# Cross-attention row maxima taken over two PSUM banks at a time: four banks for these scores, two for the transposed ones

## The chip, the cores and the metric

The kernel runs on one core of a Trainium2 chip. The core has five engines that work side by side: TensorE (PE in the profile, its weight loads PEld), VectorE (DVE), ScalarE (ACT), GpSimd (POOL) and SyncE (SP), which here only issues transfers. Matmul results go to PSUM, which has eight banks of 512 fp32 columns on 128 partitions. The metric is the device time of one launch in microseconds (us); less is better.

## What is computed

One decoder layer in fp32 on 4 sequences of 512 tokens and 512 channels: causal self-attention, cross-attention on a context of 512 tokens and 128 channels, and a feed-forward part with eight experts and a shared one. Each is added to its input. The change touches only the cross-attention:

```
def _L0_xattn_ref(q, k, v):          # q: layernorm(x), k = v = ctx_512
    H, KV = (32, 8)                  # 32 query heads on 8 key/value heads
    D = E // H                       # 16 channels a head
    qh = q.reshape(B, S, KV, G, D).transpose(0, 2, 3, 1, 4)      # G = 4
    kh = k.reshape(B, S, KV, D).transpose(0, 2, 1, 3)
    vh = v.reshape(B, S, KV, D).transpose(0, 2, 1, 3)
    scores = jnp.einsum('bkgsd,bktd->bkgst', qh, kh) / scale
    weights = jax.nn.softmax(scores, axis=-1)
    out = jnp.einsum('bkgst,bktd->bkgsd', weights, vh)
    return out.transpose(0, 3, 1, 2, 4).reshape(B, S, E)
x = x + _L0_xattn_ref(_layernorm(x, axis=-1), ctx_512, ctx_512)
```

## The kernel before

The program has three stages that follow each other: self-attention (four groups of heads), cross-attention, feed-forward. Each engine has its own instruction list, written out in full; semaphores order them against each other.

Cross-attention is cut into 32 items (`ITEMS`), one for each of 4 sequences and 8 key/value heads. An item has four query heads and four tiles of 128 tokens. The softmax needs, for each query row, the maximum over 512 keys, and this maximum is found in a pass of its own. So an item has two kinds of score matmuls. Sixteen matmuls of the first kind, written `s` (`score`, line 1180, rows `ps<-k,q` of the profile), put queries on partitions, one 128x512 block in one PSUM bank each. VectorE takes the row maximum of a block (`maximum`, line 1750, a 128x512 reduce to 128x1, `xmax`). GpSimd splits the maxima of an item into a high and a low part (`xm`, lines 986 and 989), TensorE turns them (the "m" turn), ScalarE copies them, and two transfers put them as extra rows under the queries. Sixteen matmuls of the second kind, written `st` (line 1293, rows `ps<-q,k`), then compute the scores again with keys on partitions and the maximum already subtracted; ScalarE takes the exponential of each block (line 1545, `xp`), and these feed the products with the values (`pv`, line 1303, four heads side by side, eight hardware instructions for each of the four `pv` of an item).

The order of work around the change is that of `cross_steps(m)`. An item has eight steps k = 0..7. A step has on TensorE: one `s`, two `st`, one `s`; behind that in steps 2, 4 and 6 a turn (the maxima of item m+1; in step 4 of every second item the queries; in step 6 the output of item m-2); and in the odd steps one `pv` of item m-1. The `s` run 28 blocks (`S_FIRST`) ahead, so the `s` in item m belong to items m+1 and m+2, and the last 28 blocks have no `s` beside them. The two heads of a pair lie on partitions 0 and 64, so an `s` and the `st` next to it can use the two halves of the array at the same time.

PSUM banks in this stage: `XST` = 0..2 for `st` (block n in bank n % 3), `XS` = 3..5 for `s` (block u in bank 3 + u % 3), 6 for `pv`, 7 for turns. A bank comes free in this way: before `s` number u TensorE waits until u-2 maxima are done (`s_xmax`), and before `st` number n until n-2 exponentials are done (`s_xe`). VectorE waits for the `s` of each block (`s_xs`), ScalarE for each `st` (`s_st`). Beside the maxima VectorE divides the outputs (lines 1898 and 1880, in step 6) and, in some items, normalises rows for the next sequence or for the feed-forward part (`norm_piece`: lines 198, 207, 217 to 220, 1735), one piece behind the maxima of a step. The first 28 `s` run in the self-attention stage, in banks of that stage, with one maximum each.

Of the kernel before, what the change touches and what calls it, by code (L numbers as in the profile page):

```python
# [6 lines left out]
P = 128  # L7
ALU = mybir.AluOpType
ACT = mybir.ActivationFunctionType
AX_X = mybir.AxisListType.X  # L10
# [265 lines left out]
def score_of(u):  # L276

    return u // 8 * 2 + u % 2, u % 8 // 2
# [136 lines left out]
def build(nc, x, ctx_in, w_qkv_t, w_proj_t, gate_t, w1_t, w2_t, w3_t, kinds, out):  # L415
# [11 lines left out]
    with ExitStack() as whole:  # L427
# [110 lines left out]
        s_back = [sem(f"s_back{n}") for n in range(8)]  # L538
        s_mix = sem("s_mix")
        H1, H2, HT, HY, TURN, LOGIT, RANK = 0, 1, 2, 3, 5, 7, 7  # L540
        XST, XS, XO, XT = 0, 3, 6, 7

        pa = ExitStack()

# [541 lines left out]
        def _(pe):  # L1086
# [85 lines left out]
            def score(u, bank):  # L1172

                m = u // S_UNITS
                if u % S_UNITS == 0:
                    pe.wait_ge(s_xk3[m % KV // (KV // 2)], 32 * (m // KV + 1))
                    pe.wait_ge(s_xq3[m % 4], 32 * (m // 4 + 1))
                h, i = score_of(u % S_UNITS)
                rows = half_of(h, X_PART)
                pe.matmul(ps[:, bank, :], q3[rows, m % 4, h // 2, i * P:(i + 1) * P].bitcast(F32R),  # L1180
                          k3[rows, m % KV, :].bitcast(F32R), start=True, stop=True).then_inc(s_xs, 1)
# [81 lines left out]
            def cross(m):  # L1263
                for op in cross_steps(m):
                    if op[0] == "t":
                        kind, n = op[1:]

                        at = X_TURNS.index((kind, n))
                        if X_TURNS[at - 1][0] == "o":
                            pe.wait_ge(s_od, X_TURNS[at - 1][1] + 1)  # L1270
                        else:
                            pe.wait_ge(s_ta, taken(*X_TURNS[at - 1]))
                        if kind != "o":
                            turn_up(kind, n)
                        else:
                            pe.wait_ge(s_oe, n + 1)
                            for i in range(TOK_TILES):
                                ins = turned(pe, ps[:, XT, i * P:(i + 1) * P], o_t[:, n % 2, i * P:(i + 1) * P],
                                             ident[:, :])
                            ins.then_inc(s_ot, 1)  # L1280
                    elif op[0] == "s":
                        u = op[1]
                        pe.wait_ge(s_xmax, max(S_FIRST, u - 2))
                        score(u, XS + u % 3)
                    elif op[0] == "st":
                        h, t, n = block_of(op[1])
                        if n == 0:
                            pe.wait_ge(s_m3[m % 2], 32 * (m // 2 + 1))
                        n += S_UNITS * m
                        if n >= 3:  # L1290
                            pe.wait_ge(s_xe, n - 2)
                        rows = half_of(h, X_ROWS)
                        pe.matmul(ps[:, XST + n % 3, :], k3[rows, m % KV, t * P:(t + 1) * P].bitcast(F32R),  # L1293
                                  q3[rows, m % 4, h // 2, :].bitcast(F32R), start=True, stop=True).then_inc(s_st, 1)
                    elif op[0] == "pv":
                        j, n = op[1], m - 1
                        if j == 0:
                            pe.wait_ge(s_vx, n // KV + 1)
                            if n:
                                pe.wait_ge(s_oe, n)  # L1300
                        pe.wait_ge(s_xe, S_UNITS * m - 2 * (TOK_TILES - 1 - j))
                        for h in range(XG):
                            ins = pe.matmul(ps[VW * h:VW * (h + 1), XO, :], vx[:, n // KV % 2, n % KV, j, :],  # L1303
                                            xp[:, n % 2, h, j, :], start=(j == 0), stop=(j == TOK_TILES - 1),
                                            tile_position=(0, VW * h))
                        if j == TOK_TILES - 1:
                            ins.then_inc(s_xpv, 1)
# [140 lines left out]
        def _(act):  # L1448
# [90 lines left out]
            def cross(m):  # L1539
                for op in cross_steps(m):  # L1540
                    if op[0] == "st":
                        h, t, n = block_of(op[1])
                        n += S_UNITS * m
                        act.wait_ge(s_st, n + 1)
                        act.activation(xp[:, m % 2, h, t, :], ps[:, XST + n % 3, :], ACT.Exp,  # L1545
                                       scale=X_SCALE).then_inc(s_xe, 1)
                    elif op[0] == "t" and op[1] != "o":
                        take_turned(op[1], op[2])
                    elif op == ("pv", TOK_TILES - 1):
                        act.wait_ge(s_xpv, m)  # L1550
                        act.copy(o_t[:, (m - 1) % 2, :], ps[:, XO, :]).then_inc(s_oe, 1)
# [86 lines left out]
        def _(dve):  # L1638
# [105 lines left out]
            def maximum(u, bank):  # L1744
                m = u // S_UNITS
                h, i = score_of(u % S_UNITS)
                if u % S_UNITS == 0 and m >= 2:
                    dve.wait_ge(s_ml, m - 1)
                dve.wait_ge(s_xs, u + 1)
                dve.tensor_reduce(xmax[:, m % 2, h % 2, h // 2, i:i + 1], ps[:, bank, :], AX_X, ALU.max,  # L1750
                                  negate=True).then_inc(s_xmax, 1)

            def low_turned(g, op, t):

                i = op[1] % TOK_TILES
                dve.wait_ge(s_te, turns_done(g, t) + 1)
                dve.tensor_tensor(ptl[:, i:4 * i + 1:3, :],  # L1757
                                  ps[:, T_BANK + (1 + t) % 2, 0:(i + 1) * P].rearrange("p (j n) -> p j n", n=P),
                                  pth[:, i:4 * i + 1:3, :].bitcast(F32), ALU.subtract).then_inc(s_tl, 1)
# [124 lines left out]
            def cross(m):  # L1884
                pending = None
                for op in cross_steps(m):
                    if op[0] == "s":
                        maximum(op[1], XS + op[1] % 3)
                    if op[0] in ("s", "end") and pending is not None:
                        divide(*pending)  # L1890
                        pending = None
                    if op[0] == "end" and m < ITEMS:
                        norm_piece(m // KV, m % KV, op[1])
                    if op[:2] == ("t", "o"):
                        n = op[2]
                        dve.wait_ge(s_ot, n + 1)
                        o = ps[:, XT, :].rearrange("p (g d) -> p g d", d=VW)
                        pending = n, count.mark(dve.reciprocal(xrec[:, :], o[:, :, XD]))
# [222 lines left out]
```

## Time and profile before

| what | us |
|---|---|
| time, median of 3 runs (lowest, highest) | 1870.25 (1852.72, 1870.81) |
| profiled execution, its own time | 1844.48 |
| its span, from the first to the last instruction | 1842.6 |
| PE busy / DVE busy / ACT busy in the span | 1731.1 / 1210.5 / 918.4 |
| DVE in the maxima of cross-attention (line 1750, 512 instructions) | 320.8 |
| ACT in the exponentials of cross-attention (line 1545, 512 instructions) | 273.4 |

The profile shows the profiled execution, which is one run. Busy time is the sum of instruction durations of an engine; the durations of two neighbours overlap at their ends, so that back to back they start closer together than one of them lasts. Matmul ends are modelled, so a busy PE is not PE at its peak. Starts of instructions are the surer thing to read.

### The profile page before, as it was taken

What the parts mean: (1) busy time and instruction counts of PE and PEld (TensorE: products, weight loads), DVE (VectorE), ACT (ScalarE), POOL (GpSimd) and SP (SyncE); (2) the same over time, 40 slices, a digit from 0 to 9 for tenths busy, and PEclk for the clock granted to TensorE, in tenths of its full rate; (3) what the DMA queues carried; (4) which work ended last, traced back from release to release, by engine and by line L of the source; (5) the groups of instructions that cost most, each with busy time, mean ns of one, the idle gap of its engine ahead of it and who ended that gap; (6) DMA issues with size and microseconds to landing.
All of it is one profiled execution on the core that took longest, in us unless ns stands there. A gap on an engine that the chain in (4) does not pass through costs nothing.

```text
span 1842.6 us, 26550 instructions
## 1 busy us (share of the span) xinstructions
PE 1731.1 (94%) x9753; PEld 1327.8 (72%) x9753; DVE 1210.5 (66%) x2477; ACT 918.4 (50%) x1937; POOL 182.5 (10%) x299
## 2 busy tenths in 40 slices
PE   5799999999999999998799999998899999999998
PEld 4688888888888888886533333333399999999997
DVE  6656666556655656666488999999245246766766
ACT  2444444444434444433167777787432136666641
POOL 1000000000000000002032323121012400000024
PEclk9899999999999999998679999999679999999999
DMA  4000100010000100004023444442201357878746
GB/s 149 1 1 7 29 1 24 1 29 7 24 1 7 29 2 23 1 2 124 1 86 88 135 124 137 128 133 72 89 10 67 129 186 273 300 270 299 267 150 227
DMA packets 103203, 167.21 MB, mean 91 GB/s; under 512 B 8324, under 2 KB 52356, under 8 KB 102308
## 3 DMA queue, kind: packets, MB, share of 16 engines
q1 hardware_dynamic: 97956, 148.74, 24.9%
q0 software_dynamic: 5120, 16.78, 2.7%
q8 instruction: 79, 1.29, 0.3%
q14 instruction: 48, 0.39, 0.1%
HBM read 116.15 MB, written 49.28 MB: 90 GB/s over the span
## 4 chain that ended last, share of the span: by engine, by line
PE 77%; DVE 18%; ACT 3%; issue 2%; POOL 1%; DMA 0%; POOLq 0%; ACTq 0%
PE ps L181 37%; DVE xmax L1750 9%; PE ps L187 8%; PE ps L1418 8%; PE ps L1224 7%; PE ps L1119 5%; PE ps L1303 4%; PE ps L1180 3%; PE ps L1293 2%; DVE nmax L1718 1%; DVE stats L198 1%; DVE al L1765 1%; PE ps L1354 1%; DVE probs L1726 1%; ACT ah L1523 1%
## 5 line engine op out<-in xcount | busy, mean ns | idle before, releaser
L1750 DVE TENSOR_REDUCE xmax<-ps 128x1 f32<-128x512 f32 x512 | 320.8, 683 | 39.4 <-PE ps L1180 38.7
L1545 ACT ACTIVATE xp<-ps 128x512 f32<-128x512 f32 x512 | 273.4, 603 | 102.8 <-PE ps L1293 101.8
L1478 ACT ACTIVATE probs<-ps,nmax 128x128 f32<-128x128 f32 (+3 forms) x256 | 135.9, 531 | 169.2 <-DVE nmax L1718 169.2
L1180 PE MATMUL ps<-k,q 48*128 48x512 f32 x512 | 207.7, 484 | 7.5 <-DVE xmax L1750 4.2
L1293 PE MATMUL ps<-q,k 50*128 50x512 f32 x512 | 200.5, 480 | 4.9 <-ACT xp L1545 4.9
L1180 PEld LDWEIGHTS ps<-k,q 48*128 48x128 f32 x512 | 87.0, 194 | 145.2 <-DVE xmax L1750 113.6
L1518 ACT CAST pth<-ps 128x128 fp32r<-128x128 f32 (+3 forms) x256 | 108.5, 424 | 89.8 <-PE ps L187 89.8
L1303 PE MATMUL ps<-xp,vx 128*32 128x512 f32 x1024 | 147.4, 652 | 0.8 <-issue 0.8
L1718 DVE TENSOR_REDUCE nmax<-ps 128x1 f32<-128x128 f32 (+3 forms) x256 | 123.6, 483 | 12.4 <-PE ps L1119 11.0
L1757 DVE TENSOR_TENSOR ptl<-ps,pth 128x128 fp32r<-128x128 f32 (+3 forms) x256 | 123.9, 484 | 0.0
L181 PE MATMUL ps<-w12h,x_h 128*128 128x352 f32 x568 | 121.2, 335 | 0.0
L1765 DVE TENSOR_TENSOR al<-ps,ah 128x512 fp32r<-128x512 f32 x64 | 44.3, 691 | 116.8 <-ACT ah L1523 116.8
L187 PE MATMUL ps<-ident,probs 128*128 128x128 f32 x640 | 113.6, 276 | 7.3 <-DVE ptl L1757 4.7
L181 PE MATMUL ps<-w12h,x_l 128*128 128x352 f32 x568 | 116.1, 327 | 0.0
L181 PE MATMUL ps<-w12l,x_h 128*128 128x352 f32 x568 | 115.6, 326 | 0.0
L181 PE MATMUL ps<-xh,wh 128*128 128x512 f32 x384 | 110.6, 411 | 2.1 <-DVE wl L1696 2.1
L1923 DVE TENSOR_TENSOR w12l<-w_raw,w12h 128x1408 fp32r<-128x1408 f32 x56 | 90.7, 1620 | 27.9 <-ACT w12h L1576 27.9
L1726 DVE TENSOR_SCALAR probs<-probs,rinv 128x128 f32<-128x128 f32 (+3 forms) x256 | 100.8, 394 | 9.1
L1293 PEld LDWEIGHTS ps<-q,k 50*128 50x128 f32 x512 | 81.8, 196 | 34.1 <-ACT xp L1545 24.5
L181 PE MATMUL ps<-xh,wl 128*128 128x512 f32 x384 | 105.5, 397 | 0.0
L187 PEld LDWEIGHTS ps<-ident,probs 128*128 128x128 f32 x640 | 82.1, 142 | 32.0 <-DVE probs L1726 7.0
L181 PE MATMUL ps<-xl,wh 128*128 128x512 f32 x384 | 104.6, 395 | 0.0
(191 smaller groups left out, 3550.6 us busy)
## 6 DMA issues: line engine op xcount, KB each, us to landing
w_raw<-in_w_t SPq DMA_DIRECT2D x56, 704.0 KB, 6.0
w_raw<-in_w_t SPq DMA_DIRECT2D x28, 768.0 KB, 5.9
q<-q_way SPq DMA_DIRECT2D x64, 192.0 KB, 3.2
rows_x<-w_raw SPq DMA_DIRECT2D x39, 256.0 KB, 3.4
mixed<-rows_x SPq DMA_DIRECT2D x39, 256.0 KB, 4.4
rows_y<-y_s SPq DMA_DIRECT2D x39, 256.0 KB, 5.5
q_way<-q_hi SPq DMA_DIRECT2D x32, 256.0 KB, 4.5
w_raw<-in_w_qkv_t SPq DMA_DIRECT2D x24, 256.0 KB, 2.9
```

The source lines that it names most:

```text
L181: last = pe.matmul(dst, lhs, rhs, start=(n == 0), stop=(n == len(pairs) - 1))
L187: return pe.matmul(dst, src, ident, start=True, stop=True, is_transpose=True)
L1180: pe.matmul(ps[:, bank, :], q3[rows, m % 4, h // 2, i * P:(i + 1) * P].bitcast(F32R), k3[rows, m % KV, :].bitcast(F32R), start=True, stop= ...
L1224: ins = pe.matmul(ps[:, O_BANK + h % 2, j * P:], v[:, b % 2, j, :], p[:, 4 * j:3 * j + TOK_TILES, :].rearrange("p i n -> p (i n)"), start= ...
L1293: pe.matmul(ps[:, XST + n % 3, :], k3[rows, m % KV, t * P:(t + 1) * P].bitcast(F32R), q3[rows, m % 4, h // 2, :].bitcast(F32R), start=True ...
L1303: ins = pe.matmul(ps[VW * h:VW * (h + 1), XO, :], vx[:, n // KV % 2, n % KV, j, :], xp[:, n % 2, h, j, :], start=(j == 0), stop=(j == TOK_ ...
L1418: ins = pe.matmul(ps[:, HY + n % 2, :], lhs, rhs, start=(step.opens and m == 0), stop=(step.closes and m == len(pairs) - 1))
L1478: act.activation(probs[u % 4][:, 0:w], ps[:, S_BANK + u % 2, 0:w], ACT.Exp, bias=nmax[:, u % 4:u % 4 + 1], accum_out=rsum[:, u % 4:u % 4 + ...
L1545: act.activation(xp[:, m % 2, h, t, :], ps[:, XST + n % 3, :], ACT.Exp, scale=X_SCALE).then_inc(s_xe, 1)
L1718: dve.tensor_reduce(nmax[:, u % 4:u % 4 + 1], ps[:, S_BANK + u % 2, 0:w], AX_X, ALU.max, negate=True).then_inc(s_max, 1)
L1750: dve.tensor_reduce(xmax[:, m % 2, h % 2, h // 2, i:i + 1], ps[:, bank, :], AX_X, ALU.max, negate=True).then_inc(s_xmax, 1)
L1757: dve.tensor_tensor(ptl[:, i:4 * i + 1:3, :], ps[:, T_BANK + (1 + t) % 2, 0:(i + 1) * P].rearrange("p (j n) -> p j n", n=P), pth[:, i:4 * ...
```

## The change

The two `s` of a step now go to two neighbouring banks, and one VectorE instruction (`two_maxima`, new) reduces both: input 128x2x512, output 128x2, and it counts `s_xmax` up by two. For this the `s` get four banks (2..5, block u in bank 2 + u % 4) and the `st` two (0 and 1, block n in bank n % 2). TensorE waits for maxima only before the first `s` of a step, for the same count as before. Before `st` number n it now waits until n-1 exponentials are done, one more than before. The first 28 maxima are still taken one at a time.

```diff
-        XST, XS, XO, XT = 0, 3, 6, 7
+        XST, XS, XO, XT = 0, 2, 6, 7
...
                     elif op[0] == "s":
                         u = op[1]
-                        pe.wait_ge(s_xmax, max(S_FIRST, u - 2))
-                        score(u, XS + u % 3)
+                        if u % 2 == 0:
+
+                            pe.wait_ge(s_xmax, max(S_FIRST, u - 2))
+                        score(u, XS + u % 4)
                     elif op[0] == "st":
                         h, t, n = block_of(op[1])
                         if n == 0:
                             pe.wait_ge(s_m3[m % 2], 32 * (m // 2 + 1))
                         n += S_UNITS * m
-                        if n >= 3:
-                            pe.wait_ge(s_xe, n - 2)
+                        if n >= 2:
+                            pe.wait_ge(s_xe, n - 1)
                         rows = half_of(h, X_ROWS)
-                        pe.matmul(ps[:, XST + n % 3, :], k3[rows, m % KV, t * P:(t + 1) * P].bitcast(F32R),
+                        pe.matmul(ps[:, XST + n % 2, :], k3[rows, m % KV, t * P:(t + 1) * P].bitcast(F32R),
                                   q3[rows, m % 4, h // 2, :].bitcast(F32R), start=True, stop=True).then_inc(s_st, 1)
...
-                        act.activation(xp[:, m % 2, h, t, :], ps[:, XST + n % 3, :], ACT.Exp,
+                        act.activation(xp[:, m % 2, h, t, :], ps[:, XST + n % 2, :], ACT.Exp,
                                        scale=X_SCALE).then_inc(s_xe, 1)
...
+            def two_maxima(u):
+
+
+                m = u // S_UNITS
+                h, i = score_of(u % S_UNITS)
+                if u % S_UNITS == 0 and m >= 2:
+                    dve.wait_ge(s_ml, m - 1)
+                dve.wait_ge(s_xs, u + 2)
+                bank = XS + u % 4
+                dve.tensor_reduce(xmax[:, m % 2, :, h // 2, i], ps[:, bank:bank + 2, :], AX_X, ALU.max,
+                                  negate=True).then_inc(s_xmax, 2)
...
                 for op in cross_steps(m):
-                    if op[0] == "s":
-                        maximum(op[1], XS + op[1] % 3)
+                    if op[0] == "s" and op[1] % 2:
+                        two_maxima(op[1] - 1)
```

How TensorE's list stands in steps 4 and 5 of item 1, before (`s` is line 1180, `st` line 1293, the turn line 187, `pv` line 1303):

```order
L1180 MATMUL ps<-k,q 128x512 [waits s_xmax]
L1293 MATMUL ps<-q,k 128x512 [waits s_xe] x2
L1180 MATMUL ps<-k,q 128x512 [waits s_xmax]
L187 MATMUL ps<-ident,ctx_p 128x128 [waits s_cp,s_ta]
L187 MATMUL ps<-ident,ctx_p 128x128 x3
L1180 MATMUL ps<-k,q 128x512 [waits s_xmax]
L1293 MATMUL ps<-q,k 128x512 [waits s_xe] x2
L1180 MATMUL ps<-k,q 128x512 [waits s_xmax]
L1303 MATMUL ps<-xp,vx 32x512 [waits s_xe]
L1303 MATMUL ps<-xp,vx 32x512 x3
```

The same place now (`st` is line 1295, `pv` line 1305):

```order
L1180 MATMUL ps<-k,q 128x512 [waits s_xmax]
L1295 MATMUL ps<-q,k 128x512 [waits s_xe] x2
L1180 MATMUL ps<-k,q 128x512
L187 MATMUL ps<-ident,ctx_p 128x128 [waits s_cp,s_ta]
L187 MATMUL ps<-ident,ctx_p 128x128 x3
L1180 MATMUL ps<-k,q 128x512 [waits s_xmax]
L1295 MATMUL ps<-q,k 128x512 [waits s_xe] x2
L1180 MATMUL ps<-k,q 128x512
L1305 MATMUL ps<-xp,vx 32x512 [waits s_xe]
L1305 MATMUL ps<-xp,vx 32x512 x3
```

No matmul has moved. The second `s` of a step has lost its wait, and the two waits for exponentials before the `st` stand where they stood, each for one exponential more.

VectorE's list from step 5 to the end of an item that normalises query rows, before (maxima are line 1750):

```order
L1735 TENSOR_SCALAR xn<-res,mv,rstd 128x4x8x16 [waits s_qt]
L1750 TENSOR_REDUCE xmax<-ps 128x1 [waits s_xs] x2
L1898 RECIPROCAL xrec<-ps 128x16 [waits s_ot]
L1880 TENSOR_TENSOR xo<-ps,xrec 128x256 [waits s_dve]
L1750 TENSOR_REDUCE xmax<-ps 128x1 [waits s_xs] x2
L1735 TENSOR_SCALAR xn<-res,mv,rstd 128x4x8x16
```

The same place now (maxima are line 1764):

```order
L1737 TENSOR_SCALAR xn<-res,mv,rstd 128x4x8x16 [waits s_qt]
L1764 TENSOR_REDUCE xmax<-ps 128x2 [waits s_xs]
L1912 RECIPROCAL xrec<-ps 128x16 [waits s_ot]
L1894 TENSOR_TENSOR xo<-ps,xrec 128x256 [waits s_dve]
L1764 TENSOR_REDUCE xmax<-ps 128x2 [waits s_xs]
L1737 TENSOR_SCALAR xn<-res,mv,rstd 128x4x8x16
```

Two reduces have become one with two outputs; everything else stands between the same steps as before.

## Rows read from the trace of the kernel before

**Rows 1.** Page, part 2: TensorE's granted clock in 40 slices of 46 us.
```profile
PEclk9899999999999999998679999999679999999999
```

**Rows 2.** Page, part 4: the chain that ended last, by line.
```profile
PE ps L181 37%; DVE xmax L1750 9%; PE ps L187 8%; PE ps L1418 8%; PE ps L1224 7%; PE ps L1119 5%; PE ps L1303 4%; PE ps L1180 3%; PE ps L1293 2%; DVE nmax L1718 1%; DVE stats L198 1%; DVE al L1765 1%; PE ps L1354 1%; DVE probs L1726 1%; ACT ah L1523 1%
```

**Rows 3.** Waits, 920 to 1316 us: waiter, awaited, us in total, times, longest.
```profile
PEld ps L1180 <- DVE xmax L1750: 109.7, 174, 1.7
...
ACT xp L1545 <- PE ps L1293: 101.1, 139, 17.6
```

**Rows 4.** Timeline of POOL, line 986, once an item: start, us, instruction, idle before.
```profile
922.69 0.22 POOL L986 TENSOR_TENSOR xm<-xmax,ones 128x16 fp32r<-128x16 f32 x1 [42.88 <-DVE xmax L1750]
...
977.50 0.22 POOL L986 TENSOR_TENSOR xm<-xmax,ones 128x16 fp32r<-128x16 f32 x1 [3.14 <-DVE xmax L1750]
...
1023.29 0.22 POOL L986 TENSOR_TENSOR xm<-xmax,ones 128x16 fp32r<-128x16 f32 x1 [2.40 <-DVE xmax L1750]
...
1073.34 0.22 POOL L986 TENSOR_TENSOR xm<-xmax,ones 128x16 fp32r<-128x16 f32 x1 [2.86 <-DVE xmax L1750]
...
1119.12 0.21 POOL L986 TENSOR_TENSOR xm<-xmax,ones 128x16 fp32r<-128x16 f32 x1 [2.86 <-DVE xmax L1750]
...
1237.88 0.21 POOL L986 TENSOR_TENSOR xm<-xmax,ones 128x16 fp32r<-128x16 f32 x1 [2.86 <-DVE xmax L1750]
...
1277.84 0.22 POOL L986 TENSOR_TENSOR xm<-xmax,ones 128x16 fp32r<-128x16 f32 x1 [4.74 <-DVE xmax L1750]
1291.13 0.22 POOL L986 TENSOR_TENSOR xm<-xmax,ones 128x16 fp32r<-128x16 f32 x1 [3.66 <-DVE xmax L1750]
```

**Rows 5.** Timeline, steps 4 to 7 of one item, 1064.4 to 1070.3 us.
```profile
1064.52 0.50 PE L1180 MATMUL ps<-k,q 48*128 48x512 f32 x1
...
1065.09 2.07 ACT L1545 ACTIVATE xp<-ps 128x512 f32<-128x512 f32 x4 [0.58 <-PE ps L1293]
...
1065.74 0.49 PE L1293 MATMUL ps<-q,k 50*128 50x512 f32 x1 [0.24 <-ACT xp L1545]
...
1066.23 1.07 PE L1303 MATMUL ps<-xp,vx 128*32 128x512 f32 x8
1067.22 0.50 PE L1180 MATMUL ps<-k,q 48*128 48x512 f32 x1
...
1068.48 0.50 PE L1180 MATMUL ps<-k,q 48*128 48x512 f32 x1
...
1070.15 0.50 PE L1180 MATMUL ps<-k,q 48*128 48x512 f32 x1
```

**Rows 6.** DVE: groups by form (busy us, mean ns), then two rows of its timeline.
```profile
L1750 DVE TENSOR_REDUCE xmax<-ps 128x1 f32<-128x512 f32 x512 | 320.8, 683 | 39.4 <-PE ps L1180 38.7
...
L1718 DVE TENSOR_REDUCE nmax<-ps 128x1 f32<-128x128 f32 x64 | 18.0, 282 | 0.0
...
1059.66 0.74 DVE L1735 TENSOR_SCALAR xn<-res,mv,rstd 128x512 f32<-128x512 f32 x1
...
1069.59 3.67 DVE L1750 TENSOR_REDUCE xmax<-ps 128x1 f32<-128x512 f32 x6
```

**Rows 7.** Timelines of PE and ACT in the last items, where no `s` is left.
```profile
1306.01 1.22 PE L1293 MATMUL ps<-q,k 50*128 50x512 f32 x3
...
1306.84 2.08 ACT L1545 ACTIVATE xp<-ps 128x512 f32<-128x512 f32 x4 [1.99 <-PE ps L1293]
...
1307.48 0.79 PE L1293 MATMUL ps<-q,k 50*128 50x512 f32 x1 [0.26 <-ACT xp L1545]
...
1308.21 1.94 PE L1303 MATMUL ps<-xp,vx 128*32 128x512 f32 x8
1310.07 1.22 PE L1293 MATMUL ps<-q,k 50*128 50x512 f32 x3
```

**Rows 8.** Windows: stretch, its us, busy PE, PEld, DVE, ACT, POOL, PEclk, DMA.
```profile
1264.00:1277.84 13.84, 11.96 (x69) 4.76 (x69) 13.63 (x33) 9.98 (x20) 2.13 (x4) 1.00 0.17 50
...
1292.00:1318.00 26.00, 24.97 (x91) 7.25 (x90) 2.49 (x8) 14.56 (x28) 2.08 (x3) 0.52 0.28 88
```

## The prediction, made before the changed kernel had run

> **What bounds the kernel now.** The chain that ended last comes first: 9% of the span is VectorE's maxima, and TensorE's cross-attention matmuls (lines 1180, 1293, 1303) stand beside them with 9% [rows 2]. So the stage is shared between VectorE and TensorE. The waits inside it agree: TensorE's weight loads stand 109.7 us behind maxima, in 174 places, while the exponentials have spare time, since ScalarE waits 101.1 us for the `st` [rows 3]. Taken alone this speaks for the change: it makes VectorE's work cheaper and gives up a bank where ScalarE seems to have time.
>
> The wait table overstates it, since a weight load also "waits" while the array is still busy with `pv`. The timeline of starts shows the truth. Two steps, from the `s` that opens an even step to the next such `s`, take 1067.22 - 1064.52 = 2.70 us where no turn is in them, and 1070.15 - 1067.22 = 2.93 us with a turn [rows 5]. In the first case one `st` was late because of an exponential, although it had three banks: the exponentials start 0.57 us behind the opening `s`, the first lasts some 0.60, and the fourth `st` starts at 1065.74, which is 0.57 + 0.60 + 0.05 = 1.22 behind 1064.52 [rows 5]. So the `st` ring already touches the path with three banks.
>
> How long items take is read from GpSimd's instruction that comes once an item [rows 4]. Four kinds: (a) quiet items, without normalising: 977.50 to 1023.29 and 1073.34 to 1119.12, four each, 11.45 us an item; 1119.12 to 1237.88 is one busy group and six more quiet ones at the same pace; 14 in all, at about two alternating lengths of which 11.45 is the mean. (b) Two busy groups of four, 50.05 us each (1023.29 to 1073.34). (c) The three before 1277.84, 39.96 us, with VectorE busy 13.63 of 13.84 us in the last of them [rows 8]. (d) The first four, 54.81 us, partly at half clock, one at the end (13.29), and behind it the tail without `s`.
>
> **The change part by part.**
>
> *The maxima.* A reduce of 128 columns takes 282 ns, one of 512 takes 683: 1.044 ns a column. A pair of 1024 columns would take 683 + 512 x 1.044 = 1.22 us. Six in a row of 512 span 3.67 us, so they start (3.67 - 0.68)/5 = 0.60 apart, and a pair should follow the next one after 0.60 + 0.53 = 1.13 us instead of 1.20 [rows 6]. The gain is 0.07 us a pair, 0.53 us of VectorE's time an item; for the 242 pairs 16 us if every bit were on the path. The Trainium skill, page "VectorE: DVE Perf Modes", section on the trn2 errata, has the same shape, a fixed cost and one cycle a column at 0.96 GHz; by it the pair saves only the fixed cost of one instruction, and the trace's slope agrees.
>
> *The waits of `s`.* A pair may only start when both `s` are there, some 0.34 us later than the first maximum did, and it frees two banks at once. With two pairs of banks this costs nothing in quiet items: pair p must end before the opening `s` of step p+2, which is a whole two-step (2.7 us or more) behind its own, and it ends 0.79 + 1.22 = 2.0 us behind that. I take zero.
>
> *The `st` ring, two banks for three.* This is the term that decides. Call T the opening `s` of an even step. The exponentials of its two `st` start at T + 0.57 and T + 1.06 (four of them span 2.07, so they start 0.49 apart) and end at T + 1.17 and T + 1.66 [rows 5]. With two banks the third `st` waits for the first exponential, T + 1.22, and the fourth for the second, T + 1.66 + 0.05 = T + 1.71. In the row of now `pv` starts 0.49 behind such a late `st` (1065.74 to 1066.23), since the late `st` and the last `s` no longer overlap their start-up with the step before, and the next opening `s` comes 0.99 behind `pv` (1066.23 to 1067.22). So a two-step takes 1.71 + 0.50 + 0.99 = 3.20 us, turn or no turn: a turn now ends at T + 1.26 [rows 5], within the time that the step waits anyway. Without a turn that is +0.50 against 2.70, with one +0.27 against 2.93. The `pv` in the odd step gives ScalarE 1 us to catch up, so the next even step starts without a debt. An item is 4 x 3.20 = 12.80 us, and 0.05 more for the copy of the output that delays the exponentials of step 0: 12.85, to be compared with 11.45. Behind the waiting `st` stand the last `s`, the pair maximum, the turn of the maxima and `pv`: all of TensorE's list shifts with it.
>
> *Quiet items:* 14 x (12.85 - 11.45) = **+19.6 us**.
>
> *Busy groups.* Without normalising they could not take less than 4 x 12.85 = 51.4; the normalising pieces of step 0 (three of four items have one) delay the pair of step 1 and with it the turn of the maxima, each by at most its own length, 0.74 for a query tile [rows 6]: 51.4 + 2.2 = 53.6. Now 50.05. VectorE has more room than before, so I take the middle, 52.5: 2 x 2.45 = **+4.9**.
>
> *The three items of (c):* bounds are 39.96 less 3 x 0.53 (VectorE sets the pace) and 3 x (12.85 + 0.74) = 40.8. Nearest to the upper end, since all three carry the same waits: **+0.6**. *First four and the one at half clock:* at half clock TensorE itself takes longer than the ring, and the first item has no `pv`; bounds 0 and 5 x 1.4; I take **+1.9**.
>
> *The tail.* At half clock four `st` start a two-step; the exponentials start 0.83 behind, the fourth `st` comes at 1.47, `pv` at 2.20, the next one at 4.06 [rows 7]. With two banks the third `st` moves to 1.47 and the fourth one exponential further, 1.96: +0.49 in each of four two-steps without a turn and about +0.2 in two with one: **+2.4**.
>
> Sum: 19.6 + 4.9 + 0.6 + 1.9 + 2.4 = **+29.4 us**. The profiled execution took 1844.48 us and would take about 1874. It lies 25.8 us below the median of the runs, 1870.25, and nothing in the trace says where that comes from; the same sum on the median gives **1900 us**.
>
> **The rivals.**
>
> *R1, faster: VectorE is the bound.* If the ring did not bind (if `st` found free banks because `pv` lies between), only the saved 0.07 us a pair would be left, 16 us, and up to 0.3 us an item of TensorE's waits for the second maximum of a step, 8 us: 1870 - 16 to -24, say 1850. For it: the 109.7 us of waits on maxima [rows 3] and stretches like 1264 to 1277.84 where VectorE is never idle [rows 8]. Against it: the four `st` of a two-step stand in front of its `pv`, not around it. It decides if the fourth `st` starts before T + 1.6.
>
> *R2, within 1%: the ring costs half.* If the late `st` keeps its overlap, `pv` follows 0.34 behind it (the distance of two pairs of matmuls), and busy stretches gain on VectorE what they lose on the ring: two-steps of 3.04, quiet items of 12.2, 14 x 0.75 = 10.5, the rest about 3: 1884.
>
> *R3, much slower: the clock falls.* The granted clock is at or near full speed in cross-attention except at its two ends [rows 1]; it is 0.52 in the tail [rows 8]. Now TensorE will pause in each two-step. At half clock a two-step takes 4.06 and more [rows 7]; if a third of 30 items ran so, 10 x 4 x 0.9 = 36 us come on top: 1936. Against it: items of 13.84 us, with longer pauses than the 12.85 forecast, ran at clock 1.00 [rows 8]. The Trainium skill, page "TensorE: Matmul & The Clock Gate", section on psum-queue depth-cycling, speaks against this change: a kernel whose TensorE idles briefly as it cycles through PSUM banks saw its clock swing between half and full. By that rule the time would be R3's; no run here shows it for pauses this short.
>
> **How the numbers follow.** The ring as worked out 0.75, R2 0.12, R1 0.06, R3 0.07. About 1% is what a measurement of this kernel can tell from no change, so slower means above 1889. Of the first case, whose own range is 1886 to 1915, a small part falls within 1%: slower 0.78, within 1% 0.17, faster 0.05. The range reaches down to R2, whose runs may also lie as low as the lowest one before, and up past the upper bounds of the open terms (busy groups +2.2, first items +5, a few items at half clock): 1872 to 1920.
>
> **What would show each step.** The pair maximum lasts 1.2 us, and VectorE's busy time in maxima falls by some 30 us. GpSimd's item mark comes every 12.8 to 12.9 us in quiet items. Waits of `st` (line 1295) for exponentials grow by some 30 to 40 us in total; waits of `s` for maxima shrink. All items alternate no longer, since a turn costs nothing. The clock stays 1.0 in quiet items. The prediction is wrong if quiet items stay below 12.2, if `pv` starts less than 2.1 us behind the opening `s`, if pairs take far over 1.3 us, or if the clock falls between 980 and 1240 us.

## The result

| | median us (lowest to highest) | runs |
|---|---|---|
| before | 1870.25 (1852.72 to 1870.81) | 3 |
| changed | 1896.45 (1892.38 to 1906.51) | 3 |
| ratio | 1.0192, 95% interval 1.015 to 1.0234 | |

The change makes the kernel slower, by 26 us between the medians. A second comparison on another occasion (e0 below) gave 1.0231 (1.0179 to 1.0283). The profiled execution of the changed kernel took 1892.38 us, with a span of 1890.5; that of before had 1842.6. The page of the changed kernel:

```profile
span 1890.5 us, 26515 instructions
...
PEclk9999999999999999996789999899898899999999
...
PE ps L181 35%; PE ps L187 9%; PE ps L1420 7%; PE ps L1224 7%; PE ps L1119 5%; PE ps L1305 5%; PE ps L1180 4%; PE ps L1295 4%; DVE xmax L1764 4%; DVE nmax L1720 1%; DVE al L1779 1%; PE ps L1356 1%; DVE probs L1728 1%; DVE stats L198 1%; DVE ptl L1771 1%
...
L1764 DVE TENSOR_REDUCE xmax<-ps 128x2 f32<-128x1024 f32 x242 | 295.4, 1221 | 67.5 <-PE ps L1180 66.0
```

The 242 pairs last 1221 ns each, as the slope of [rows 6] said, and the maxima's share of the chain fell from 9% [rows 2] to 4%. TensorE's cross-attention lines took over the share: 9% became 13%. VectorE's relief is small, though: its busy time in the maxima went from 320.8 us to 313.3 (295.4 in the pairs, 17.9 in the 28 single ones at the start), not down by some 30 us as forecast.

The item marks of GpSimd, to be held against [rows 4]:

```profile
918.45 0.22 POOL L986 TENSOR_TENSOR xm<-xmax,ones 128x16 fp32r<-128x16 f32 x1 [41.89 <-DVE xmax L1764]
...
978.31 0.22 POOL L986 TENSOR_TENSOR xm<-xmax,ones 128x16 fp32r<-128x16 f32 x1 [3.46 <-DVE xmax L1764]
...
1028.64 0.21 POOL L986 TENSOR_TENSOR xm<-xmax,ones 128x16 fp32r<-128x16 f32 x1 [2.85 <-DVE xmax L1764]
...
1081.58 0.21 POOL L986 TENSOR_TENSOR xm<-xmax,ones 128x16 fp32r<-128x16 f32 x1 [3.31 <-DVE xmax L1764]
...
1132.21 0.22 POOL L986 TENSOR_TENSOR xm<-xmax,ones 128x16 fp32r<-128x16 f32 x1 [3.32 <-DVE xmax L1764]
...
1190.08 0.21 POOL L986 TENSOR_TENSOR xm<-xmax,ones 128x16 fp32r<-128x16 f32 x1 [5.43 <-DVE xmax L1764]
...
1266.79 0.21 POOL L986 TENSOR_TENSOR xm<-xmax,ones 128x16 fp32r<-128x16 f32 x1 [3.31 <-DVE xmax L1764]
...
1320.05 0.21 POOL L986 TENSOR_TENSOR xm<-xmax,ones 128x16 fp32r<-128x16 f32 x1 [3.77 <-DVE xmax L1764]
```

| stretch between marks | before | changed | difference | forecast |
|---|---|---|---|---|
| first four items | 54.81 | 59.86 | +5.1 | +1.9 with the last item |
| quiet items, 14 | 160.3 | 177.7 | +17.4 | +19.6 |
| two busy groups of four | 100.1 | 110.8 | +10.7 | +4.9 |
| three items of (c) and the last one | 53.25 | 53.26 | 0.0 | +0.6 |
| all 30 intervals | 368.4 | 401.6 | +33.2 | |

The first mark comes 4.2 us earlier, and from the last mark to the end it is 570.5 us against 551.5, 19 us more. That last figure is not the change's, as e0 will show. In the quiet items one of 13.75 us is counted whose first part ran at half clock; without it the mean is 12.6 us.

How a two-step looks now, TensorE from 1093.7 to 1106.3 us:

```profile
1096.80 0.49 PE L1180 MATMUL ps<-k,q 48*128 48x512 f32 x1
1096.80 0.73 PE L1295 MATMUL ps<-q,k 50*128 50x512 f32 x2
...
1098.01 0.98 PE L1295 MATMUL ps<-q,k 50*128 50x512 f32 x2 [0.23 <-ACT xp L1547]
1098.50 0.50 PE L1180 MATMUL ps<-k,q 48*128 48x512 f32 x1
1098.93 1.07 PE L1305 MATMUL ps<-xp,vx 128*32 128x512 f32 x8
1099.92 0.50 PE L1180 MATMUL ps<-k,q 48*128 48x512 f32 x1
...
1103.06 0.50 PE L1180 MATMUL ps<-k,q 48*128 48x512 f32 x1
...
1106.25 0.49 PE L1180 MATMUL ps<-k,q 48*128 48x512 f32 x1
```

With T = 1096.80 the third `st` starts at T + 1.21, the fourth with the last `s` at T + 1.70, `pv` at T + 2.13, the next two-step at T + 3.12. The two that follow take 3.14 (a turn is in it) and 3.19 (none is, but the copy of the output). So a turn costs nothing any more, and an item is 12.58 us. `pv` stands 0.43 us behind the last score matmul (1098.50 to 1098.93).

### The profile page after: what moved, and what is told of

Its sections match the earlier page's. It is cut to its first block, busy times and chain, and to the rows that moved or that the text cites. A ratio compares the mean times of both kernels' runs of the same rounds, so it can differ in the third digit from the quotient of the medians.

```text
span 1890.5 us, 26515 instructions
## 1 busy us (share of the span) xinstructions
PE 1747.6 (92%) x9753; PEld 1323.9 (70%) x9753; DVE 1204.7 (64%) x2235; ACT 923.8 (49%) x1937; POOL 182.1 (10%) x299
## 4 chain that ended last, share of the span: by engine, by line
PE 78%; DVE 13%; issue 4%; ACT 3%; POOL 1%; another core or an unknown queue 1%; DMA 0%; DVEq 0%; POOLq 0%; ACTq 0%
PE ps L181 35%; PE ps L187 9%; PE ps L1420 7%; PE ps L1224 7%; PE ps L1119 5%; PE ps L1305 5%; PE ps L1180 4%; PE ps L1295 4%; DVE xmax L1764 4%; DVE nmax L1720 1%; DVE al L1779 1%; PE ps L1356 1%; DVE probs L1728 1%; DVE stats L198 1%; DVE ptl L1771 1%
## 5 line engine op out<-in xcount | busy, mean ns | idle before, releaser
L1764 DVE TENSOR_REDUCE xmax<-ps 128x2 f32<-128x1024 f32 x242 | 295.4, 1221 | 67.5 <-PE ps L1180 66.0
L1547 ACT ACTIVATE xp<-ps 128x512 f32<-128x512 f32 x512 | 278.8, 598 | 114.4 <-PE ps L1295 109.9
L1180 PE MATMUL ps<-k,q 48*128 48x512 f32 x512 | 217.6, 495 | 6.7 <-DVE xmax L1764 3.3
L1295 PE MATMUL ps<-q,k 50*128 50x512 f32 x512 | 217.9, 491 | 6.0 <-ACT xp L1547 5.8
L1305 PE MATMUL ps<-xp,vx 128*32 128x512 f32 x1024 | 142.9, 633 | 0.8 <-issue 0.8
L1720 DVE TENSOR_REDUCE nmax<-ps 128x1 f32<-128x128 f32 (+3 forms) x256 | 123.3, 482 | 12.1 <-PE ps L1119 10.7
L1295 PEld LDWEIGHTS ps<-q,k 50*128 50x128 f32 x512 | 86.5, 193 | 57.4 <-ACT xp L1547 54.2
L181 PEld LDWEIGHTS ps<-w12h,x_h 128*128 128x128 f32 x568 | 96.1, 192 | 16.2 <-issue 9.5
```

The lines of the kernel that those rows point to most:

```text
L181: last = pe.matmul(dst, lhs, rhs, start=(n == 0), stop=(n == len(pairs) - 1))
L1295: pe.matmul(ps[:, XST + n % 2, :], k3[rows, m % KV, t * P:(t + 1) * P].bitcast(F32R), q3[rows, m % 4, h // 2, :].bitcast(F32R), start=True ...
L1547: act.activation(xp[:, m % 2, h, t, :], ps[:, XST + n % 2, :], ACT.Exp, scale=X_SCALE).then_inc(s_xe, 1)
L1720: dve.tensor_reduce(nmax[:, u % 4:u % 4 + 1], ps[:, S_BANK + u % 2, 0:w], AX_X, ALU.max, negate=True).then_inc(s_max, 1)
L1764: dve.tensor_reduce(xmax[:, m % 2, :, h // 2, i], ps[:, bank:bank + 2, :], AX_X, ALU.max, negate=True).then_inc(s_xmax, 2)
```

## The experiments

All kernels but e2 and e3 compute the whole layer. "Ratio" is against the kernel before, run on the same occasion; medians of different occasions are not comparable (before had 1832, 1837 and 1867 us on the three: e0 to e3, e4 to e6, e7 to e9). A quiet item is read from the marks of one profile. e2 and e3 were run once each (1847.62 and 1828.55 us) and serve for their traces only.

| | median us | ratio (95% interval) | quiet item us |
|---|---|---|---|
| before | | 1 | 11.45 |
| e0 changed kernel again | 1872.54 | 1.0231 (1.0179 to 1.0283) | 12.60 |
| e1 banks of the change, single maxima | 1851.93 | 1.0106 (1.0064 to 1.0148) | 12.60 |
| e6 four banks for `st`, two for `s`, single maxima | 1861.90 | 1.0162 (1.011 to 1.0215) | 13.27 |
| e4 before, `pv` cut in two | 1869.09 | 1.0188 (1.013 to 1.0246) | 11.97 |
| e5 changed, `pv` cut in two | 1916.57 | 1.045 (1.0383 to 1.0517) | 12.85 |
| e7 changed, two query tiles later | 1883.59 | 1.0107 (1.0056 to 1.0158) | 12.59 |
| e8 changed, all normalising pieces later | 1879.23 | 1.008 (1.0047 to 1.0112) | 12.59 |
| e9 before, all normalising pieces later | 1857.51 | 0.9939 (0.9907 to 0.9971) | 11.45 |

### e0: does it repeat?

No edit; the changed kernel.

> The changed kernel once more, profiled and timed against the kernel before on the same chip. Its first profile was 47.9 us longer than that of before, of which 33 us lay in the cross-attention items and 19 us behind the last of them, in feed-forward work that the change does not touch. Ring theory: the items repeat to within 2 us (quiet items 12.58 us, 401 us from the first to the last item mark, but for dips of the clock), and the 19 us behind them do not repeat. Rival (the change lengthens the feed-forward part through its phase or its transfers): they repeat within 5 us.

From the first to the last mark it took 399.88 us (920.74 to 1320.62). The last mark and the span of its page:

```profile
span 1859.2 us, 26515 instructions
...
1320.62 0.22 POOL L986 TENSOR_TENSOR xm<-xmax,ones 128x16 fp32r<-128x16 f32 x1 [3.75 <-DVE xmax L1764]
```

Behind it lie 538.6 us, against 570.5 in the first profile of the same program. So 32 us of feed-forward time come and go without any edit. A part of it shows in the first profile of the changed kernel as pauses of TensorE, of which this is the longest:

```profile
1454.10 1.54 PE L181 MATMUL ps<-w12h,x_h 128*128 128x352 f32 x4 [7.69 <-issue]
```

"Issue" is a wait for nothing that the profile shows; the matmuls behind it last nearly twice as long, at a granted clock of 0.50. The profiles of before and of e0 to e6 have no such row; those of e7, e8 and e9 have one each (5.4, 6.9 and 5.9 us). So it is not the change's either: e9 has the banks of before. What it is stays open. The 47.9 us between the first two spans are therefore 33 us between the marks and a remainder of accident. The medians lie only 26 us apart, and the profiled execution of before was 25.8 us faster than the median of its runs; whether those runs had such pauses no trace shows.

### e1: the banks alone

```diff
-        XST, XS, XO, XT = 0, 3, 6, 7
+        XST, XS, XO, XT = 0, 2, 6, 7
-                        pe.wait_ge(s_xmax, max(S_FIRST, u - 2))
-                        score(u, XS + u % 3)
+                        pe.wait_ge(s_xmax, max(S_FIRST, u - 3))
+                        score(u, XS + u % 4)
-                        if n >= 3:
-                            pe.wait_ge(s_xe, n - 2)
+                        if n >= 2:
+                            pe.wait_ge(s_xe, n - 1)
...          st in bank XST + n % 2, maximum(op[1], XS + op[1] % 4)
```

> The kernel before with only the banks of the change: two banks for the transposed scores (st), four for the scores (s), but still one maximum a block and one wait a block. Ring theory: quiet items take 12.5 to 12.7 us as in the changed kernel, and the whole kernel is as slow as it, within 6 us. Rival (the pair costs: it starts later, lasts 1.22 us and frees two banks at once): quiet items take 11.3 to 11.5 us as before.

```profile
1104.16 0.50 PE L1180 MATMUL ps<-k,q 48*128 48x512 f32 x1
...
1105.43 0.99 PE L1293 MATMUL ps<-q,k 50*128 50x512 f32 x2 [0.31 <-ACT xp L1545]
1105.92 0.50 PE L1180 MATMUL ps<-k,q 48*128 48x512 f32 x1
1106.35 1.06 PE L1303 MATMUL ps<-xp,vx 128*32 128x512 f32 x8
1107.35 0.49 PE L1180 MATMUL ps<-k,q 48*128 48x512 f32 x1
```

The same 3.19 us and the same places as in the changed kernel, without a single pair. Quiet items are 12.60 us. The ring of two is shown as the cause of the loss in quiet items. But the whole kernel is only 1.1% slower than before, not 2.3% as e0 on the same occasion: the medians are 20.6 us apart, where I had expected 6 at most. So pairing has a price of its own, outside the quiet items. The two profiles show 6.3 us of it between the first and the last mark (399.88 us in e0, 393.55 in e1). A busy group in which the clock does not fall takes 52.94 us with pairs (the changed kernel's first), 51.47 with single maxima (e1's second) and 50.05 before. The rest lies in executions that were not profiled: three of e0's four had a mean granted clock of 0.955 to 0.962, e1's four 0.967 to 0.970.

### e2 and e3: the exponentials cut to half

Both leave out half of each exponential: 256 of 512 columns are computed, and `pv` reads them twice. The edit is the same in both:

```diff
-                        act.activation(xp[:, m % 2, h, t, :], ps[:, XST + n % 2, :], ACT.Exp,
+                        act.activation(xp[:, m % 2, h, t, 0:SEQ // 2], ps[:, XST + n % 2, 0:SEQ // 2], ACT.Exp,
-                                            xp[:, n % 2, h, j, :], start=(j == 0), stop=(j == TOK_TILES - 1),
+                                            xp[:, n % 2, h, j, 0:SEQ // 2].unsqueeze(1).to_broadcast([P, 2, SEQ // 2]), start=(j == 0), stop=(j == TOK_TILES - 1),
```

> The changed kernel with half of each exponential of cross-attention left out (256 of 512 columns; the products with the values read that half twice, so TensorE's work is the same). An exponential should last 0.39 us instead of 0.60. Ring theory: the fourth st is free at about T + 1.3 instead of T + 1.71, the ring no longer binds, TensorE sets the pace: quiet items about 10.8 to 11.1 us. Rival (the pair costs): quiet items stay above 12 us, since nothing about the maxima has changed.

> The kernel before with the same half of each exponential left out. With three st banks the ring hardly bound: only the two-steps without a turn gain. Both theories: quiet items 11.1 to 11.4 us, held by single maxima at 0.60 us each. Read against e2_after_half_exp it tells what pairing is worth where the ring does not bind: by the ring theory e2 is faster than this by 0.2 to 0.5 us an item; by the rival it is slower by a microsecond.

The exponentials last 384 ns. Quiet items: 11.57 us with the change's banks and pairs (11.68 and 11.46 in turn), 11.44 with the kernel before. TensorE in e2:

```profile
1086.79 0.50 PE L1180 MATMUL ps<-k,q 48*128 48x512 f32 x1
...
1089.49 0.50 PE L1180 MATMUL ps<-k,q 48*128 48x512 f32 x1
...
1093.40 0.50 PE L1180 MATMUL ps<-k,q 48*128 48x512 f32 x1 [0.25 <-DVE xmax L1764]
...
1096.71 0.27 PE L187 MATMUL ps<-ident,xm 128*32 128x128 f32 x1 [0.79 <-POOL xm L989]
```

A shorter exponential takes 1.0 us from the item and a two-step is back at 2.70. The rival, that the pair itself holds quiet items above 12 us, is out. But the items were expected at 10.8 to 11.1 us in e2 and at 11.1 to 11.4 in e3; both are longer. Where the ring does not bind, pairing is not 0.2 to 0.5 us faster: it is 0.13 slower. In the rows two things wait for a late pair: the turn of the maxima (0.79 us here) and, once, an `s` (0.25).

e3 tells one thing more: on the kernel before, the shorter exponential gains nothing, 11.44 us against 11.45. TensorE in e3, in a two-step without a turn:

```profile
1101.03 0.50 PE L1180 MATMUL ps<-k,q 48*128 48x512 f32 x1
...
1102.40 0.50 PE L1180 MATMUL ps<-k,q 48*128 48x512 f32 x1
...
1103.82 0.50 PE L1180 MATMUL ps<-k,q 48*128 48x512 f32 x1
```

The last `s` starts 1.37 us behind the opening one, right behind the maximum that it waits for (that one ends at 1102.34), and the two-step takes 2.79. Before, with full exponentials, the same two lengths are 1.38 and 2.81 (from 1104.58 us). So with three banks the wait for an exponential cost nothing; the last `s`, held by a maximum, comes just as late without it.

### e4 and e5: pv spread over both steps

```diff
-        if 1 <= m <= ITEMS and k % 2:
-            ops.append(("pv", k // 2))
+        if 1 <= m <= ITEMS:
+            ops.append(("pv", k // 2, k % 2))
...          half = op[2]; output and right operand cut to 256 columns, start=(j == 0 and half == 0)
```

> The kernel before, with each product with the values (pv, 1.0 us on TensorE in every odd step) cut into two halves of 256 query columns, one in each step; same work, same result. It spreads the st evenly, so an exponential has a whole step of about 1.17 us before its bank is wanted (it needs 1.22 less 0.34), and the maxima too. Ring theory: waits for exponentials and maxima vanish, TensorE's own time is left: quiet items 10.8 to 11.1 us instead of 11.45, the stage 10 to 15 us shorter. Rival (what binds is TensorE, and cutting costs it twice the weight loads of pv): items of 11.5 to 12.5 us.

> The changed kernel with the same cut of pv. If the cost of two st banks comes from four st standing in front of one pv, spreading must give part of it back: steps may not follow each other faster than 1.22 us (0.57 + 0.60 + 0.05 for one bank), so quiet items of 11.6 to 12.3 us instead of 12.58. Rival (ring cost does not depend on where pv stands): 12.6 us or more.

Both went the rival's way (11.5 to 12.5 us was its range for e4, 12.6 or more for e5). TensorE in e4:

```profile
1108.37 0.27 PE L187 MATMUL ps<-ident,xm 128*32 128x128 f32 x1 [0.58 <-POOL xm L989]
1108.57 0.64 PE L1304 MATMUL ps<-xp,vx 128*32 128x256 f32 x8
1109.14 0.50 PE L1180 MATMUL ps<-k,q 48*128 48x512 f32 x1
```

A half takes 0.57 us on the path (1108.57 to 1109.14), so a whole one costs 1.14 instead of 0.99, 0.6 us an item; no `st` waits any more, as foreseen, but TensorE waits longer at the turn of the maxima (0.58 us against 0.32 before). The items became 11.97 and 12.85 us. In e5 too no `st` stands behind an exponential for more than 0.1 us between 975 and 1235 us, so its 12.85 us are not the ring's; since the cut has a price of its own, the two runs do not say what spreading `pv` would be worth without it. In addition the clock fell more often: 18 us at a granted clock of 0.53 in one place of e4 (1063 to 1081 us), and nine items of 17 to 19.4 us in e5, where the turn of the maxima waits 1.22 to 2.09 us at seven places between 945 and 1245 us.

### e6: the mirror image

```diff
-        XST, XS, XO, XT = 0, 3, 6, 7
+        XST, XS, XO, XT = 0, 4, 6, 7
...          st n in bank n % 4, waits for n - 3 exponentials; s u in bank 4 + u % 2, waits for u - 1 maxima
```

> The mirror image: four banks for st, two for s, one maximum a block. By the ring arithmetic a ring of two is too short for s as well: the last s of a two-step waits for the second maximum, 0.54 + 0.60 + 0.68 + 0.05 = 1.87 us behind the opening s, pv starts at 2.3, the next two-step at 3.3: quiet items 13.0 to 13.4 us, slower than the changed kernel. If only exponentials matter (rival: the bank of st is what counts, s has slack), quiet items are at most 11.5 us.

```profile
1100.42 0.50 PE L1180 MATMUL ps<-k,q 48*128 48x512 f32 x1 [0.54 <-DVE xmax L1750]
...
1101.01 0.50 PE L1180 MATMUL ps<-k,q 48*128 48x512 f32 x1
...
1101.44 1.07 PE L1303 MATMUL ps<-xp,vx 128*32 128x512 f32 x8
1102.44 0.49 PE L1180 MATMUL ps<-k,q 48*128 48x512 f32 x1
```

Quiet items of 13.27 us (13.0 to 13.4 forecast): the ring arithmetic holds for `s` and VectorE as well. A surprise stands beside it: its quiet items are 0.67 us longer than the changed kernel's, 9 us for the 14, yet from the first to the last mark it takes 404.3 us, only 3 to 4 us more, and its ratio is no higher (1.6% over before against 1.9 and 2.3%, intervals that overlap). It is also the only one up to here whose clock never fell between 945 and 1245 us; the stretch from 970 on:

```profile
970.00:1240.00 270.00, 248.87 (x1447) 95.70 (x1445) 229.41 (x403) 193.29 (x378) 62.04 (x106) 1.00 0.38 112
```

### e7, e8, e9: where VectorE normalises

What pairing costs beyond the ring shows in the changed kernel at the end of a busy group. Timeline of POOL and PE:

```profile
1172.25 0.63 POOL L986 TENSOR_TENSOR xm<-xmax,ones 128x16 fp32r<-128x16 f32 x1 [3.87 <-DVE xmax L1764]
...
1173.32 0.27 PE L187 MATMUL ps<-ident,xm 128*32 128x128 f32 x1 [2.08 <-POOL xm L989]
...
1174.18 1.94 PE L1305 MATMUL ps<-xp,vx 128*32 128x512 f32 x8
```

Query tiles in steps 7, 0 and 1 delay the last pair that the turn needs; TensorE stands still for 2.08 us, and within a microsecond the clock is halved (eight `pv` take 1.94 us instead of 1.07). Seventeen us follow at half clock:

```profile
1173.00:1190.00 17.00, 16.68 (x65) 5.71 (x65) 10.03 (x10) 8.44 (x16) 0.90 (x2) 0.54 0.20 57
```

The same wait was 1.20 us before the change and 1.28 in e1, where it was followed by 17 us at half clock too (from 1065.7 us). I went through all pauses of TensorE over 0.7 us between 945 and 1245 us in the profiles of before, of the changed kernel and of the ten experiments, and took the granted clock of the 4 us from 1 us behind each as the sign of a fall:

| TensorE's pause | pauses | granted clock at or below 0.70 behind it |
|---|---|---|
| 1.9 to 2.1 us | 11 | 9 |
| 1.2 to 1.6 us | 22 | 10 |
| 0.7 to 1.12 us | 67 | 1 |

Of these 100 pauses 85 stand at a turn of the maxima, the others at an `s`. The ring's waits in full items are shorter, 0.23 and 0.31 us in the rows shown. In the twelve profiles no stretch of half clock there began without a pause of this table right ahead of it. e6, which has no pause over 0.7 us there, has no fall either; that fits its surprise.

This holds for that stretch alone. In the kernel before, in the feed-forward part, the granted clock was 1.00 from 1354.7 to 1361.5 us and 0.50 in the 3.4 us behind, with no pause of TensorE over 0.24 us in either. What else precedes a fall no run here tells.

e7 moves the two query tiles only (the first pair of lines, on the changed kernel), e8 and e9 make all five edits (on the changed kernel and on that of before):

```diff
-QUERY_AT = [(2, 5), (2, 7), (3, 0), (3, 1)]
+QUERY_AT = [(2, 5), (2, 7), (3, 3), (3, 5)]
...
-                    if 3 <= kv < 6 and k == 0:
+                    if 3 <= kv < 6 and k == 2:
...
-                    if 5 <= kv and k == 0:
+                    if 5 <= kv and k == 4:
...
-                if (kv, k) == (1, 0):
+                if (kv, k) == (1, 2):
...
-                if (kv, k) == (2, 0):
+                if (kv, k) == (2, 2):
```

> The changed kernel with two of the four query tiles of VectorE moved from steps 0 and 1 of the item before the end of a busy group to its steps 3 and 5. In the changed kernel the turn of the maxima waits 2.08 us behind them (1.20 before the change), and in its profiles the granted clock fell to 0.5 right behind such a wait in two of three places. Pause theory: the wait shrinks below 1 us, the third busy item goes from 13.97 to 12.9 to 13.2 us, the items of 14 to 18 us (half clock) vanish in the middle of the stage, and the kernel gains 6 to 15 us on the changed one. Rival (the falls of the clock have nothing to do with this pause): items of 16 to 18 us stay, and the gain is 2 to 3 us (three items, 0.9 us each).

> As e7, and the other pieces that stand at step 0 (aggregation of the moments, reciprocal roots) moved to step 2 or 4, so that nothing but maxima stands before the turn of the maxima in steps 0 and 1. Ring theory: busy items approach the quiet ones, 12.6 to 12.9 us each, busy groups 51 us instead of 52.9; with the pause theory the kernel is 10 to 18 us faster than the changed one, and still slower than the kernel before by 15 us or more, since the ring is untouched.

> The kernel before with the same moves as e8: a candidate that would beat both. VectorE's work is unchanged and sets the pace of busy items, so busy groups stay near 49.5 to 50 us; the pause of 1.20 us goes. Pause theory: the half-clock stretch at the start of the stage (item of 14.3 us) shrinks, the kernel is 2 to 6 us faster than before. Rival: no difference within 2 us.

e7's ratio is 1.011, where the changed kernel had 1.019 and 1.023 on other occasions; it was not run again beside e7 to e9. The third busy item went from 13.98 to 13.35 us and its wait from 2.08 to 1.08, both a little above what I expected, and from the fourth item to the 26th none is longer than 13.4. Of the stage's 399.9 (e0) or 401.6 us, 388.8 are left; the items that merely got shorter explain about 3 of these 11 to 13 us, the rest was half clock. e8 took the stage to 384.3 us and the ratio to 1.008; its window from 970 to 1240 us:

```profile
970.00:1240.00 270.00, 254.03 (x1522) 91.64 (x1521) 230.34 (x249) 203.67 (x398) 63.52 (x110) 1.00 0.42 122
```

The ring's short waits are all still in this kernel (quiet items 12.59), and the clock is 1.00 throughout. Between e8 and before 12 us are left between the medians, where I had expected 15 at least. But before has its own pauses of 1.20 us and e8 has not. The fair partner is e9, with the banks of before and the same places for VectorE's pieces: 21.7 us between the medians of the same occasion, and 384.3 against 362.05 us from the first to the last mark. So some 22 us are what the banks and pairs cost together where the clock does not fall: neither profile has a fall from 945 us to the last mark.

e9 is faster than the kernel before: 0.9939 (0.9907 to 0.9971), 9.7 us between the medians (10 runs against 17), more than the 2 to 6 expected. A busy group takes 49.52 us (1019.44 to 1068.96) against 50.05, the whole stage 362.05 against 368.44, and from 945 us on no turn of the maxima waits over 0.8 us. Each of e7, e8 and e9 was profiled once; that the falls went with the long pauses rests on these three profiles and the table.

```profile
1019.44 0.22 POOL L986 TENSOR_TENSOR xm<-xmax,ones 128x16 fp32r<-128x16 f32 x1 [2.39 <-DVE xmax L1750]
...
1068.96 0.22 POOL L986 TENSOR_TENSOR xm<-xmax,ones 128x16 fp32r<-128x16 f32 x1 [2.85 <-DVE xmax L1750]
```

## Why the prediction was right, and where it was not

The time, 1896.45 us, lies 3.6 us from the 1900 forecast and on the side forecast, and the main mechanism is the one named. One of its own signs of being wrong came true all the same: the clock fell between 980 and 1240 us. Point by point:

- **The price of a pair**: right. 1.22 us forecast, 1221 ns measured. The sign given for it was wrong: VectorE's busy time in maxima fell by 7.5 us, not by some 30. The prediction's own gain of 0.07 us a pair makes 16 us; even that did not come.
- **The ring of two banks**: right in mechanism (e1, e2), a little too dear. The third and fourth `st` start where they were put, T + 1.21 and T + 1.70. The term that was off is the step from the late `st` to `pv`, taken as 0.50 from 1065.74 and 1066.23 [rows 5]. TensorE has one more row between them:

```profile
1065.80 0.50 PE L1180 MATMUL ps<-k,q 48*128 48x512 f32 x1
```

`pv` stands 0.43 behind this last `s`, there as in the changed kernel, where the last `s` starts together with the fourth `st`. For the same reason the prediction was wrong that the ring already touched the path with three banks (e3); it did no harm to the sum, since a two-step was taken at its measured 2.70. So the two-step is 3.14 us and not 3.20, the item 12.58 and not 12.85, and the 14 quiet items cost 17.4 instead of 19.6 us, one of them at half clock in part.

- **Pairing costs nothing**: right only for the opening `s`, which was the one wait that I looked at. The turn of the maxima waits for the last pair of an item, and a pair is done later than a single maximum. In quiet items the ring covers this (e2 uncovers it, 0.13 us). In busy items it does not.
- **Busy groups**: the step that failed. Forecast was the middle of two bounds, 2.45 us a group. The first took +2.9, within the bounds; the second +7.8 (57.87 us where 53.6 was the upper bound), since the bounds counted VectorE's pieces and not what a longer pause of TensorE can set off. The second group holds the stretch of 17 us above. This is a piece of R3 that happened: the clock fell, though not from the ring's waits, and not for a third of the items, but for one or two behind a pause of 2 us.
- **First four items**: +5.1 where 1.9 was taken. Their third item ends with the same pause of 2.08 us, and the granted clock behind it was 0.50.
- **The tail**: the +0.5 us a two-step is there. At full clock it is 2.60 us with three banks (e9) and 3.10 with two:

e9, TensorE:
```profile
1293.66 0.73 PE L1293 MATMUL ps<-q,k 50*128 50x512 f32 x3
1294.84 0.49 PE L1293 MATMUL ps<-q,k 50*128 50x512 f32 x1 [0.45 <-ACT xp L1545]
...
1296.26 0.73 PE L1293 MATMUL ps<-q,k 50*128 50x512 f32 x3
```

Changed kernel, TensorE:
```profile
1331.70 0.50 PE L1295 MATMUL ps<-q,k 50*128 50x512 f32 x2
...
1334.80 0.50 PE L1295 MATMUL ps<-q,k 50*128 50x512 f32 x2
```

But this tail ran at full clock and that of [rows 7] at half, so in these two profiles the changed kernel's tail is the shorter one, by 8.7 us up to the first pause behind it. The forecast had assumed that it would stay at half clock.

- **R1** is out: the fourth `st` starts at T + 1.70, beyond the T + 1.6 that would have decided, and without the ring there would be no gain from pairs either (e2 against e3). **R2** is out for the stage, which lost 33 us (e0 against before: 31); the late `st` loses 0.09 us of overlap, less than the 0.16 that I took and not zero. **R3**'s place was wrong: e8 keeps the ring's pauses and stays at clock 1.00 from 970 to 1240 us. The Trainium skill, section on psum-queue depth-cycling in "TensorE: Matmul & The Clock Gate", tells of a kernel whose clock swung with brief idling of TensorE between groups of matmuls. For the ring's pauses of 0.23 to 0.31 us the traces of this stage do not bear that out.

The sum was partly right by luck: the quiet items were priced 2 us too high, the busy groups and first items 9 us too low, the tail 11 us too high in these two profiles, and the accidents of the feed-forward part (28 us between the two) are larger than all of these.

## What to carry to other kernels

When a ring of buffers loses one, do not ask how much spare time its consumer has, but write down one round: start of the producer, start and end of the consumer, the semaphore, and compare it with what stands between two uses on the producer's engine. Here ScalarE was idle a quarter of the time, and with two banks its ring set the pace of the quiet items all the same.

Merging two instructions saves a fixed cost on a busy engine and delays the first result; look for whoever waits for the last result of a batch, for there the merge costs. And what stands in front of such a hand-over (here VectorE's normalising pieces) can be free to move: that alone gave 0.6% over the kernel before (e9).

## What had not been expected of the hardware

- How often a pause of TensorE in this stage was followed by half clock within a microsecond or so (the table above): 9 of 11 at 2 us, 10 of 22 at 1.2 to 1.6 us, 1 of 67 at 0.7 to 1.12 us. The same pause at the same place of the same program does it in one group of items and not in the next, so a single profile shows chance here. A fall of 10 to 17 us costs some 4 to 6 us (items of 17.8 and 13.8 us for ones of 12.9 and 12.6), a short one of under 4 us 1.3 to 1.9. Why one pause of a length does it and another does not stays open.
- The same program can lose some 30 us in the feed-forward part between two executions (538.6 and 570.5 us behind the last mark), with TensorE standing up to 7.7 us for a reason that the profile does not show; four of the twelve profiles have such a stand, the first of the changed kernel and the three of the last occasion. Two single profiles can mislead by more than this change is worth.
